# Edge counts of a graph network on TensorE: register loads by fours, one place wait per four steps, and narrow one-hots made twelve steps at a time

## The reference, cut to what matters

```python
x = x + _L0_gnn_ref(h, edge_index_t, W, a, merge_kernel)   # attention over the edges, 8 heads
h = jnp.maximum(_layernorm(x, axis=-1), 0.0)
x = x + _L1_gnn_ref(h, edge_index, w1_l, b1, w1_r, w2_l, b2, w2_r)
...
msg_sum = jax.ops.segment_sum(x[src], dst, num_segments=n)   # = counts @ x
```

## Time and profile before

| | |
|---|---|
| median of 3 runs | 5613.37 us (5609.27 to 5640.14) |
| profiled execution, its own time | 5605.08 us |
| its span (first to last instruction) | 5603.3 us |
| mean granted TensorE clock over the span | 0.712 |
| first and last matmul of the counts (L525) | 103.0 us, 588.9 us |
| first instruction of the next block | 593.7 us |

### The profile page before, as it was taken

The page is one execution under the profiler, slowest core; times in us unless marked ns, Lnnn a source line. Parts: engine busy times, 40 slices in busy tenths (PEclk is TensorE's granted clock), DMA queues, the critical chain, the costliest instruction groups (busy, mean ns, idle before and its releaser), DMA issues. The chain is left out here.

```text
span 5603.3 us, 46575 instructions
## 1 busy us (share of the span) xinstructions
PE 3079.5 (55%) x11765; PEld 1927.7 (34%) x11765; DVE 3211.7 (57%) x5607; ACT 1827.1 (33%) x2737; POOL 1842.8 (33%) x1787
## 2 busy tenths in 40 slices
PE   5777688877777776885334432441101543433564
PEld 3555333322222222553223332441001433333552
DVE  6999799999999997102132111112211854556676
ACT  1333688888888885000000000000101111111200
POOL 0000222100000000001777777754775066665200
PEclk7888899999999998997555555555555555555556
DMA  1222666544444444984214222102111011111011
GB/s 38 83 85 85 170 186 191 162 118 120 119 120 123 118 116 112 211 181 99 48 40 98 45 48 44 43 17 37 31 27 29 15 37 32 37 31 30 4 42 32
DMA packets 381011, 448.82 MB, mean 80 GB/s; under 512 B 182902, under 2 KB 249365, under 8 KB 379839
## 3 DMA queue, kind: packets, MB, share of 16 engines
q1 hardware_dynamic: 328477, 390.50, 27.0%
q0 software_dynamic: 52288, 55.34, 5.1%
HBM read 351.39 MB, written 94.23 MB: 80 GB/s over the span
## 5 line engine op out<-in xcount | busy, mean ns | idle before, releaser
L889 PE MATMUL l_sum_ps<-arena,sums 125*65 125x500 f32 (+1 forms) x2600 | 1146.0, 580 | 295.8 <-DVE arena L783 272.1
L1808 POOL DMA_INDIRECT l_rows<-table,tile_src x782 | 772.1, 987 | 508.5 <-issue 229.6
L1219 POOL DMA_INDIRECT l_rows<-hidden_rows,tile_src x782 | 806.4, 1031 | 304.9 <-issue 233.9
L772 DVE SCALAR_TENSOR_TENSOR arena<-arena,far_past 125x750 f32<-125x750 f32 (+1 forms) x800 | 859.7, 1114 | 16.5 <-DMA arena<-score_rows 16.5
L1272 PE MATMUL l_acc_ps<-l_rows,l_hot 128*125 x1612 | 389.6, 388 | 718.6 <-issue 683.3
L818 ACT ACTIVATE arena<-arena,far_left 125x750 f32<-125x750 f32 (+1 forms) x800 | 713.0, 939 | 186.0 <-DVE arena L772 186.0
L783 DVE SCALAR_TENSOR_TENSOR arena<-arena,l_turned 125x1500 f32<-125x1500 f32 (+1 forms) x400 | 711.6, 1779 | 47.9 <-ACT arena L823 47.3
L2002 PE MATMUL l_sum_ps<-l_rows,l_hot 128*128 x1962 | 482.4, 425 | 439.5 <-issue 302.1
L889 PEld LDWEIGHTS l_sum_ps<-arena,sums 125*65 125x65 f32 x2600 | 331.6, 138 | 1045.0 <-issue 534.6
L1272 PEld LDWEIGHTS l_acc_ps<-l_rows,l_hot 128*125 128x125 f32 x1612 | 367.1, 313 | 742.2 <-issue 740.3
L2002 PEld LDWEIGHTS l_sum_ps<-l_rows,l_hot 128*128 128x128 f32 x1962 | 437.7, 327 | 483.0 <-issue 480.7
(11 more groups left out here) (464 smaller groups left out, 2738.3 us busy)
## 6 DMA issues: line engine op xcount, KB each, us to landing
l_turned<-turned_counts SPq DMA_DIRECT2D x225, 328.1 KB
arena<-counts SPq DMA_DIRECT2D x17, 2843.8 KB
counts<-arena SPq DMA_DIRECT2D x125, 284.4 KB
l_turned<-turned_counts SPq DMA_DIRECT2D x75, 382.8 KB
l_attr<-edge_attr_in SPq DMA_DIRECT2D x97, 256.0 KB
arena<-counts SPq DMA_DIRECT2D x75, 328.1 KB
turned_counts<-l_turned SPq DMA_DIRECT2D x75, 328.1 KB
arena<-score_rows SPq DMA_DIRECT2D x24, 732.4 KB
```

The source lines that it names most:

```text
L772: last = v.scalar_tensor_tensor(scores(k)[:, i, :], rows[:, 1, i, :], m.far_past[:, w, h:h + 1], rows[:, 0, i, :], ALU.add, ALU.max)
L889: last = nc.tensor.matmul(sum_ps[0:F + 1, c, 0:hi - lo], h_one[:, w, :], z[k % ZS][:, lo:hi], start=(w == 0), stop=(w == W - 1))
L1219: pool.indirect_dma_start(rows[:, b % RING, t, :], None, m.hidden_rows[:, :], bass.IndirectOffsetOnAxis(ap=m.tile_src[:, k:k + 1], axis=0) ...
L1808: pool.indirect_dma_start(rows[:, t % RING3, :], None, m.table3[:, :], bass.IndirectOffsetOnAxis(ap=m.tile_src[:, t:t + 1], axis=0)).then_ ...
```

## The change

- TensorE loads `fine.slot` four numbers at a time, every 4 steps, and `fine.turn` four at a time, every 16 steps. `fine.turn` now has one entry per four steps (231 in place of 462), taken at the last of the four; TensorE waits on `slot_free` once per four steps.
- VectorE makes the narrow one-hots of 12 steps in one comparison of two tensors, 125x1500: `src_code` (now fp16, each element read 125 times) with `node_iota` (each row of 125 read 12 times). The first is made ahead of all steps; that of the next round is made after the seventh step of a round. They go into a ring of three rounds (`NARROW`), and have a semaphore of their own, `narrow_ready`, for which TensorE waits once per round.
- The wide one-hots, the matmuls, ScalarE's and SyncE's parts stay.

```diff
@@ order_edges, tables @@
-            own(v.tensor_scalar(row[:, 0:HALF], t.window_f[0:1, 1:KV:2], 1.0, None, ALU.add))
-            own(v.tensor_copy(t.turn[:, :], row[:, 0:HALF]))
+            own(v.tensor_scalar(row[:, 0:KV // AT_LOAD], t.window_f[0:1, AT_LOAD - 1:KV:AT_LOAD], 1.0, None, ALU.add))
+            own(v.tensor_copy(t.turn[:, :], row[:, 0:KV // AT_LOAD]))
@@ Count.__init__ @@
+NARROW = 3 * UV
-        self.src_hot = hot[:, UV * CW:].rearrange("p (i c) -> p i c", i=UV)
+        self.src_hot = hot[:, UV * CW:].rearrange("p (a i c) -> p a i c", a=NARROW // UV, i=UV)
+        self.narrow_ready = s.sem("narrow_ready")
@@ Count.dve @@
+        def narrow(a):
+            v.tensor_tensor(self.src_hot[:, a * UV % NARROW // UV, :, :], over(m.fine.src_code[:, a * UV:(a + 1) * UV].unsqueeze(2), (P, UV, P)),
+                            over(m.node_iota[:, :].unsqueeze(1), (P, UV, P)), ALU.is_equal).then_inc(self.narrow_ready, 1)
+        narrow(0)
         for k in range(KV):
             if k >= UV:
                 dve.wait_ge(self.count_ready, k - UV + 1)
-            v.tensor_scalar(self.pair_hot[:, k % UV, :], m.code_iota[:, :], m.fine.pair_code[:, k:k + 1], None, ALU.is_equal)
-            v.tensor_scalar(self.src_hot[:, k % UV, :], m.node_iota[:, :], m.fine.src_code[:, k:k + 1], None,
+            v.tensor_scalar(self.pair_hot[:, k % UV, :], m.code_iota[:, :], m.fine.pair_code[:, k:k + 1], None,
                             ALU.is_equal).then_inc(self.hot_ready, 1)
+            if k % UV == UV // 2 and k // UV + 1 < KV // UV:
+                narrow(k // UV + 1)
@@ Count.pe @@
         for k in range(KV):
+            if k % AT_LOAD == 0:
+                slots = self.values(mybir.EngineType.PE, m.fine.slot, k, AT_LOAD, SLOTS - 1)
+            if k % AT_LOAD ** 2 == 0:
+                turns = self.values(mybir.EngineType.PE, m.fine.turn, k // AT_LOAD, min(AT_LOAD, (KV - k) // AT_LOAD), V)
+            if k % AT_LOAD == 0:
+                pe.wait_ge(self.slot_free, turns[k // AT_LOAD % AT_LOAD])
             if k % UV == 0:
-                slots = self.values(mybir.EngineType.PE, m.fine.slot, k, UV, SLOTS - 1)
-                turns = self.values(mybir.EngineType.PE, m.fine.turn, k // 2, UV // 2, V)
+                pe.wait_ge(self.narrow_ready, k // UV + 1)
             pe.wait_ge(self.hot_ready, k + 1)
-            if k % 2 == 0:
-                pe.wait_ge(self.slot_free, turns[k % UV // 2])
```

More of the change, by code:

```diff
@@ L447, in __init__ @@
         used = DEEP * CW + 3 * N
-        hot = m.arena[0:P, used:used + UV * (CW + P) // 2].bitcast(BF16)
+        hot = m.arena[0:P, used:used + (UV * CW + NARROW * P) // 2].bitcast(BF16)
         self.pair_hot = hot[:, 0:UV * CW].rearrange("p (i c) -> p i c", i=UV)
-        self.src_hot = hot[:, UV * CW:].rearrange("p (i c) -> p i c", i=UV)
+        self.src_hot = hot[:, UV * CW:].rearrange("p (a i c) -> p a i c", a=NARROW // UV, i=UV)
         self.zeros = s.sb("zeros", [P, CW // 2], BF16)
@@ L517, in pe @@
         for k in range(KV):
+            if k % AT_LOAD == 0:
[4 more added lines that the diff above has]
+                pe.wait_ge(self.slot_free, turns[k // AT_LOAD % AT_LOAD])
             if k % UV == 0:
-                slots = self.values(mybir.EngineType.PE, m.fine.slot, k, UV, SLOTS - 1)
-                turns = self.values(mybir.EngineType.PE, m.fine.turn, k // 2, UV // 2, V)
+                pe.wait_ge(self.narrow_ready, k // UV + 1)
             pe.wait_ge(self.hot_ready, k + 1)
-            if k % 2 == 0:
-                pe.wait_ge(self.slot_free, turns[k % UV // 2])
             for c in range(2):
-                last = nc.tensor.matmul(self.ps[0:P, bass.ds(slots[k % UV], 1), c, 0:CW // 2].rearrange("p a f -> p (a f)"),
-                                        self.src_hot[:, k % UV, :], self.pair_hot[:, k % UV, c * (CW // 2):(c + 1) * (CW // 2)],
+                last = nc.tensor.matmul(self.ps[0:P, bass.ds(slots[k % AT_LOAD], 1), c, 0:CW // 2].rearrange("p a f -> p (a f)"),
+                                        self.src_hot[:, k % NARROW // UV, k % UV, :], self.pair_hot[:, k % UV, c * (CW // 2):(c + 1) * (CW // 2)],
                                         start=False, stop=True, skip_group_check=True)
@@ L2353, in program @@
                         m.fine.window_f = early_sb("fine_window_f", [128, KV])
-                        m.fine.src_code, m.fine.pair_code = (early_sb(f"fine_{n}", [P, KV]) for n in ("src_code", "pair_code"))
-                        m.fine.slot, m.fine.turn = (early_sb(f"fine_{n}", [1, k], I32) for n, k in (("slot", KV), ("turn", HALF)))
+                        m.fine.src_code, m.fine.pair_code = early_sb("fine_src_code", [P, KV], F16), early_sb("fine_pair_code", [P, KV])
+                        m.fine.slot, m.fine.turn = (early_sb(f"fine_{n}", [1, k], I32) for n, k in (("slot", KV), ("turn", KV // AT_LOAD)))
                         m.fine.counted = early_sb("fine_counted", [1, V], I32)
```

## The result

| | before | the change |
|---|---|---|
| median, 4 runs each | 5617.65 us | 5547.76 us |
| lowest and highest | 5609.27, 5640.14 | 5545.19, 5552.89 |
| ratio, 95% interval | | 0.9872 [0.9846, 0.9898] |
| profiled execution, its span | 5603.3 us | 5551.1 us |
| first and last matmul of the counts | 103.0, 588.9 us | 100.9, 515.4 us |

What follows compares the result with a forecast made beforehand. The prediction took TensorE's matmuls plus register loads to bound the count; a round falling from 6.31 to 5.33 us, times 77, gains 75 us: 5613.4 - 75 = 5538 us, range 5500 to 5580.

Steps and rivals of the forecast that it cites:

- What bounds the kernel: In the count, TensorE's matmuls followed by its register loads set the 6.31 us round; VectorE needs 5.55 and waits.
- Rival D: VectorE truly causes TensorE's idle time and loads bound nothing: gain 23 us, 5590 us; chance 0.02.
- The load of four: TensorE's register load of four numbers: 0.333 us plus 0.07 for hand-over, 3.75 loads, 1.5 us a round.
- The 24 matmuls: TensorE's matmuls of a round of 12 steps: 3.6 us at full clock, 6.5 us at half clock.
- Place waits, cost zero: TensorE's place waits, six to three a round: no cost; some 0.1 us less per dropped wait, left out of the sum.
- TensorE's round 5.1, VectorE's 5.25 the bound: Full-clock round in the count: TensorE 3.6 + 1.5 = 5.1 us, VectorE 3.62 + 1.63 = 5.25 us, which bounds.
- The clock: TensorE's granted clock in the count stays at 0.86 or more; half-clock rounds take 6.5 us, so 5.33 is taken.
- Rival B: TensorE's clock sits lower: half clock half the time, 5568 us, chance 0.07; always half clock, 5628 us, chance 0.03.
- The long comparison: VectorE's one comparison of 1500 elements a round: 1.71 us of record, 1.63 us less the overlap.
- rival A: VectorE's long comparison runs at twice the rate, 0.85 us: gain about 100 us, 5513 us; chance 0.11.
- Rival C: TensorE's loads cost by the piece, not the count: slower, 5667 or 5755 us, chance 0.08; no change, 5628, chance 0.03.
- The rest: Next stages don't change; L525 ends near 514 us, next block begins near 519, TensorE's idle time falls below 80 us.

Runs made afterwards that it cites:

- TensorE's part alone: Kernel before with only loads by fours and one place wait per four steps, narrow one-hots still one per step: count 424.3 us, ratio 0.9875.
- VectorE's alone: Changed kernel with TensorE's loads and place waits as before, narrow one-hots made twelve at a time: count 486.1 us, ratio 1.0007.
- Pair waits: Changed kernel with a place wait every second step again, turns still loaded by fours: count 456.5 us, ratio 0.9943.

## Why the prediction was right, and where not

- *What bounds the kernel*: right. TensorE's sequencer did, with its loads and waits, not VectorE, whatever the releaser said. The experiments with one part each decide it: 62 us from TensorE's part alone, none from VectorE's alone. Rival D (the releaser is right) falls with this. Of the two loads before 307.43 the first ended at 306.0 and the second at 307.2, not both at 307.1; the reading stays the same.
- *The load of four*: the median of 0.333 came out at 0.334. But the sum needs the mean, and that is 0.456 for the 287 loads inside the count. The prediction took a median from a stage with other traffic; in the count six loads of ten meet a packet of a transfer. The term was 3.75 x 0.40 = 1.5 us and is 1.92.
- *The 24 matmuls*: 3.6 us were taken from the burst before, which holds six place waits. By the sequencer's own records they are 3.13 and the three waits 0.34, together 3.46.
- *Place waits, cost zero; 0.1 us each for the sequencer left out*: mis-sized. As for stalls they cost nothing, as forecast, and the wait for `narrow_ready` has no record of its own. But each place wait takes 0.11 us of the engine that bounds; leaving out three of six was worth 0.33 us a round. Pair waits cost 42 us over the change, of which the 231 waits make 24 and the loads 20.
- *TensorE's round 5.1, VectorE's 5.25 the bound*: the step that failed. The loads were put 0.4 us too low and the waits saved were left out; the two errors partly cancel. TensorE's round is 5.38 and VectorE's 5.22, so it is still TensorE's sequencer that bounds. The forecast of 5.33 a round came near by luck: it was VectorE's 5.25, lifted for rounds at half clock, and neither was what set the time.
- *The clock*: right in direction and too cautious; it went from 0.86 to 0.99. Rival B falls. But the price given to it, 6.1 us for a round at full clock and 6.5 at half, was read from single rounds and does not hold: over the count of the kernel before, rounds without half clock took 6.48 us in the mean and those with some 6.26.
- *The long comparison*: 1.717 us against 1.71, the single rate. On rival A the runs show both sides: with one element read 125 times in a row the 1500 elements took 1.717 us, and with a step of one on both inputs 0.933, which is near 0.15 us of fixed time and half of the rest. The single rate for one repeated element in a two-source operation on 2-byte data is what the Trainium skill's Vector Engine (DVE) Microarchitecture Reference has (Performance modes), and the trace agrees. Twice the rate for a 16-bit `tensor_tensor` is what the tier table on another page of the Trainium skill has (VectorE: DVE Perf Modes, The perf-mode tier table); here it held only for the layouts without the repeated element.
- *Rival C* (a load costs by the piece, whatever its size) fell with the loads of four at 0.334. What it was built on, that 6 and 12 numbers have nearly one floor, fits the price of 0.26 us for every four numbers and 0.24 for each left over. The floor of about 600 ns for a register load in the Trainium skill (DMA: Bandwidth & Descriptors, Latency and other measured facts) is not what four numbers cost here, 0.327.
- *The rest*: the last matmul stood at 515.4 (514 forecast), the next block at 520.2 (519). TensorE's idle time fell from 140 to 104.5, not below 80, and VectorE kept 9 us of idling inside the count: these two were the signs of the wrong bound.

What stays open: what exactly in a transfer holds up a register load, and whether a table on a partition that the windows' transfers don't touch would read faster; that wasn't tried. By the fitted price, eight turns in one load, two of them unused, would also be cheaper than the six of the kernel before (0.59 against 0.82 at the floor); no run shows it.

## What to carry to other kernels

An idle gap that the profile puts down to another engine can belong to the waiting engine's own sequencer: lay the end of the gap beside the start and length of the register loads, and ask whether the named engine's first result was long there. Then look at the intervals between the sequencer's own records: one that is longer than others of its kind is a real wait, and where the sequencer bounds there are hardly any. Where a sequencer is the bound, add up everything that it handles, at the mean and not the median: each register operation, each wait though it is long fulfilled, and each load. And a change of layout that speeds up the writer of a tile has to be costed at its reader too: with a step of 24 bytes the weight loads took back all that the comparison gave.

## What the runs showed of the hardware

- A register load from SBUF on TensorE took, at the least, 0.33 us for 4 numbers, 0.59 for 8, 0.84 for 12, 1.10 for 16, but 0.82 for 6 and 1.57 for 15: 16 numbers were cheaper than 15.
- Loads on TensorE of four numbers grew from a mean of 0.47 to 0.55 us when the DMA share rose from 0.32 to 0.59.
- A weight load of 125 columns in bf16 took 0.133 us contiguous, 0.137 with a step of 4 bytes between columns and 0.313 with 24.
- A wait on a semaphore that had long been reached took 0.106 us of TensorE's sequencer, a register operation ahead of a matmul 0.124.
- The granted clock of TensorE stayed at its upper level (2.4 GHz) for the last 411 us of the change's count, in bursts of 8 matmuls with pauses up to 1.3 us. In the kernel before it fell to 1.2 GHz 30 times, each time with a pause of 2.0 to 3.2 us at the fall or shortly before; with the loads alone it fell three times at pauses of 1.1 to 1.3 us.
- At half clock the 24 matmuls of a round kept up with a sequencer that needs over 6 us for it: rounds that touch half clock took 6.26 us in the mean, the others 6.48.
